# A last fix-up loop in a two-layer graph kernel: its carry moved into one extra tile, weighting and run sums moved, a ring of ten output buffers

## The reference

```python
def _L1_gnn_ref(X, w1, w2, b, edge_weight, edge_src, edge_dst):
    X0 = jnp.einsum('ab,bc->ac', X, w1)
    X1 = jnp.einsum('ab,bc->ac', X, w2)
    msgs = X1[edge_src] * edge_weight[:, None]
    agg = jax.ops.segment_sum(msgs, edge_dst, num_segments=X.shape[0])
    return jax.nn.relu(X0 + agg + b)
...
x = _layernorm(x + _L1_gnn_ref(x, ..., edge_weight, src, dst), axis=-1)
```

## Time and profile before

| | us |
|---|---|
| median of 3 runs | 1562.85 (1562.12 to 1571.67) |
| span of the profiled execution | 1705.3 |
| VectorE busy in it | 1346.5 |
| TensorE busy | 1245.0 |
| ScalarE busy | 1225.0 |
| GpSimd busy | 1042.2 |

### The profile page before, as it was taken

The page is one execution under the profiler, slowest core; times in us unless marked ns, Lnnn a source line. Parts: engine busy times, 40 slices in busy tenths (PEclk is TensorE's granted clock), DMA queues, the critical chain, the costliest instruction groups (busy, mean ns, idle before and its releaser), DMA issues.

```text
span 1705.3 us, 34722 instructions
## 1 busy us (share of the span) xinstructions
PE 1245.0 (73%) x9184; PEld 1095.8 (64%) x9184; DVE 1346.5 (79%) x5156; ACT 1225.0 (72%) x4231; POOL 1042.2 (61%) x1182
## 2 busy tenths in 40 slices
PE   1888888888888882288877876788888876665661
PEld 1877777777777772177766766666666675554551
DVE  2777898889999998888877876799999984654653
ACT  0899999999999995077787876899999962222221
POOL 2666666555566660055555656888888846666665
PEclk9999999999999996599999997999999997787876
DMA  6899999999999996734444445899999942222221
GB/s 189 269 306 302 305 305 304 303 302 301 305 301 305 308 300 233 240 117 152 154 144 140 156 141 168 270 289 292 293 289 294 292 143 77 79 82 74 86 77 38
DMA packets 210148, 372.00 MB, mean 218 GB/s; under 512 B 36740, under 2 KB 67821, under 8 KB 208935
## 3 DMA queue, kind: packets, MB, share of 16 engines
q1 hardware_dynamic: 120822, 200.48, 37.2%
q10 hardware_dynamic: 57771, 108.12, 17.3%
q0 software_dynamic: 31360, 61.17, 13.2%
HBM read 231.39 MB, written 161.37 MB: 230 GB/s over the span
## 4 chain that ended last, share of the span: by engine, by line
ACT 36%; DVE 29%; issue 11%; another core or an unknown queue 9%; PE 9%; DMA 1%; POOL 1%; SPq 1%; DVEq 1%; ACTq 0%; POOLq 0%
ACT hout L728 10%; ACT scan_buf L728 10%; DVE stats L992 7%; DVE hpre L1238 6%; ACT big L756 4%; ACT em L688 3%; DVE big L1228 3%; DVE hpre L1314 2%; ACT lv L769 2%; PE pd L596 2%; DVE hout L1002 2%; DVE scan_buf L1002 2%; PE pd L597 2%; PE pk L619 2%
## 5 line engine op out<-in xcount | busy, mean ns | idle before, releaser
L992 DVE BATCH_NORM_STATS2 stats<-hpre 128x6 f32<-128x256 f32 x882 | 334.8, 421 | 1.8
L466 POOL DMA_INDIRECT ring_a<-in_x,gidx x196 | 185.6, 947 | 207.4 <-PE pt L556 146.7
L728 ACT ACTIVATE scan_buf<-hpre,nb,rs 128x128 f32<-128x128 f32 x686 | 292.1, 480 | 2.8 <-DVE scan_buf L1002 1.3
L728 ACT ACTIVATE hout<-hpre,nb,rs 128x128 f32<-128x128 f32 x686 | 292.2, 480 | 2.5 <-issue 1.2
L1098 DVE SCALAR_TENSOR_TENSOR hpre<-pd,beta,xg 128x128 f32<-128x128 f32 x784 | 221.3, 345 | 29.0 <-DVE beta L1091 1.0
L565 PE MATMUL pd<-w_sx,scan_buf 128*128 128x129 f32 x1568 | 229.7, 276 | 0.0
L469 POOL DMA_INDIRECT ring_b<-in_x,gidx x196 | 185.0, 944 | 60.0 <-issue 60.0
L619 PEld LDWEIGHTS pk<-w_sb,scan_buf 128*128 128x128 f32 x1568 | 211.5, 196 | 7.4
L499 POOL DMA_INDIRECT big<-h_tab,gidx x196 | 193.4, 987 | 35.0 <-POOL big L505 29.5
L619 PE MATMUL pk<-w_sb,scan_buf 128*128 128x128 f32 x1568 | 209.9, 278 | 0.0
L565 PEld LDWEIGHTS pd<-w_sx,scan_buf 128*128 128x128 f32 x1568 | 207.0, 192 | 2.7
(11 more groups left out here) (208 smaller groups left out, 3692.4 us busy)
## 6 DMA issues: line engine op xcount, KB each, us to landing
xg<-in_x SPq DMA_DIRECT2D x196, 256.0 KB
scan_buf<-in_xT SPq DMA_DIRECT2D x196, 256.0 KB
val<-h_tab SPq DMA_DIRECT2D x139, 256.0 KB
h_tab<-hout ACTq DMA_DIRECT2D x98, 256.0 KB
h_tab<-scan_buf ACTq DMA_DIRECT2D x98, 256.0 KB
out_z<-hout ACTq DMA_DIRECT2D x98, 256.0 KB
out_z<-scan_buf ACTq DMA_DIRECT2D x98, 256.0 KB
h_two<-h_tab SPq DMA_DIRECT2D x57, 256.0 KB, 9.1
```

The source lines that it names most:

```text
L466: gp.indirect_dma_start(out=ring_a[:, u, :], out_offset=None, in_=x[:, :], in_offset=bass.IndirectOffsetOnAxis(ap=gidx[:, k, 0:1], axis=0))\
L728: ins = act.activation(hout[ju][:, i * D:(i + 1) * D], hpre[:, ju, i * D:(i + 1) * D], ACT.Identity, bias=nb_of(ju, i), scale=rs_of(ju, i))
L992: ins = dve.bn_stats(stats[:, ju, i, :, :].rearrange("p j s -> p (j s)"), two)
```

## The change

- The carry leaves stage C's loop. The tiles' rows of an inherited run are no longer scattered: `sidx` is raised by 2N where `psame` is 1, so that the bounds check drops them. One **extra tile** at the end computes those rows, at most one for each partition: it gathers the run's last sum from a new DRAM table `agg_scr`, and the h row, adds the scanned carry as a further product into the same PSUM group, and does relu, norm and one scatter.
- `agg_scr` is filled by 49 stores of a quad's sums, on the SP queue, behind the loads of `xg`.
- The weighting goes from GpSimd to ScalarE (`weigh_rows`). The first eight tiles are weighted and summed in the last groups of D2, and the others in stage C's loop, two quads ahead (`KQ = 2`).
- VectorE's order in pass k is now: relu of quad k, run sums of quad k+2, statistics of quad k, normalise quad k-1.
- The normalised quads go round a ring of `UZ = 10` buffers in `val`.
- Semaphores are merged, and small tiles share memory, to make room.

```
-            for k in range(T + GL):
-                if k < T:
-                    if k >= UG:
-                        gp.wait_ge(S["agg_b2"], k - UG + 1)
-                    gp.indirect_dma_start(out=agg[:, k, :], ...)
-                j = k - GL
-                if j >= 0:
-                    gp.wait_ge(hs_in[j % UG], 16 * (j // UG + 1))
-                    gp.tensor_tensor(agg[:, j, :], agg[:, j, :], ew_t[:, j:j + 1].to_broadcast([P, D]),
-                                     ALU.mult).then_inc(S["agg_b2"], 1)
+            for k in range(T):
+                if k >= UG:
+                    gp.wait_ge(hs_in[k % UG], 16 * (k // UG))
+                gp.indirect_dma_start(out=agg[:, k, :], ...).then_inc(hs_in[k % UG], 16)
...
+            for q in range(T4 - 4):
+                scatter_quad(q)
+            gp.wait_ge(S["agg_st"], 16 * T4)
+            gp.indirect_dma_start(out=agg_x, out_offset=None, in_=agg_scr[:, :], ...).then_inc(S["x_in"], 16)
+            gp.indirect_dma_start(out=h_x, out_offset=None, in_=h_tab[:, :], ...).then_inc(S["x_in"], 16)
+            for q in range(T4 - 4, T4):
+                scatter_quad(q)
+            gp.wait_ge(S["sc"], 10)
+            gp.indirect_dma_start(out=out[:, :], ..., in_=z_x, ...).then_inc(S["x_sc"], 16)
...
+            def weigh_rows(t):
+                act.wait_ge(hs_in[t % UG], 16 * (t // UG + 1))
+                act.activation(agg[:, t, :], agg[:, t, :], ACT.Copy, scale=ew_t[:, t:t + 1]).then_inc(S["agg_b2"], 1)
...
+            for k in range(T4 + 1):
+                if k < T4:
+                    if 2 <= k:
+                        c_evict(k)
+                    for t in range(NJ * (k + KQ), min(NJ * (k + KQ + 1), T)):
+                        weigh_rows(t)
+                if k > 0:
+                    inv_std(act, ...)
...
             for k in range(T4 + 1):
-                g = k - 1
                 if k < T4:
...
-                    for i in range(NJ):
-                        t = NJ * k + i
-                        ins = dve.scalar_tensor_tensor(out=hpre[:, ku, i * D:(i + 1) * D], in0=carg, ...)
-                    ins.then_inc(S["cy_c"], 1)
...
+                    dve.scalar_tensor_tensor(out=hpre[:, ku, :], in0=pk[:, k % 2, :], scalar=0.0, in1=xg[:, ku, :],
+                                             op0=ALU.max, op1=ALU.add).then_inc(S["u_c"], 1)
+                    for t in range(NJ * (k + KQ), min(NJ * (k + KQ + 1), T)):
+                        run_sum(t)
                     dve.wait_ge(S["u_c"], k + 1)
                     pair_stats(ku, NJ // 2).then_inc(S["bn_c"], 1)
+                if k > 0:
+                    g = k - 1
+                    dve.wait_ge(S["rs_c"], g + 1)
+                    if g >= UZ:
+                        dve.wait_ge(z_sc[g % UZ], NJ * 16 * (g // UZ))
+                    normalise(lambda i: z_rows(g)[:, i * D:(i + 1) * D], ...).then_inc(S["z_c"], 1)
```

More of the change, by code:

```diff
@@ L27 @@
 NP = 1
+PADDED, FILLS, FILL_E, DROPS, R_O, DSTEPS, ROWS = range(1, 8)
 QSCALE = 1.0 / C ** 0.5
@@ L232, in gnn_kernel @@
         cumT = hpre[:, 1, 0:P + 1]
+        run_a = own[:, 0:D]
+        run_b = own[:, D:2 * D]
+        run_keepT = own[:, 2 * D:3 * D]
+        run_cumT = own[:, 3 * D:4 * D + 1]
+        h_x, agg_x, hT_x, aggT_x = (ring_a[:, i, :] for i in range(4))
+        u_x, z_x = ring_b[:, 0, :], ring_b[:, 1, :]
+        ind = far[:, :]
+        row0 = sb("row0", [P, 1], I32)
+        q_row = q_sb[:, :, :].rearrange("p a n -> p (a n)")
+        at_x = q_row[:, 0:4]
+        rows_x = q_row[:, 8:10].bitcast(I32)
+        stats_x = q_row[:, 16:22].rearrange("p (j s) -> p j s", j=2)
+        lv_x = q_row[:, 24:25]
+        rs_x = q_row[:, 32:33]
         carm = sb("carm", [P, 2 * H])
         fade = sb("fade", [P, 2 * H])
[L235 removed]
+        carn = prod[:, :, :].rearrange("p a n -> p (a n)")[:, 0:DM + H]
         S = {n: sem(n) for n in (
[L239 to L240 removed]
+            "w_in", "pad_in", "ea_cp", "ea_cp2", "z_cp", "edge_in", "setup", "ident", "wprod", "wcopy",
+            "rows_in", "issued", "drop_in", "checked", "ordered",
             "g_all", "g_iota", "g_rank", "ranked", "g_one", "g_ea", "g_out", "g_back", "g_turn",
@@ L281, in gnn_kernel, with z_rows @@
         hv_in = [sem(f"hv_in{i}") for i in range(UV)]
+        z_sc = [sem(f"z_sc{i}") for i in range(UZ)]
+        def z_rows(q):
+            i = UV + q % UZ
+            return val_row[:, i * GN:(i + 1) * GN]
         def h_rows(g):
@@ L507, in _, with scatter_quad @@
+            gp.wait_ge(S["skip_c"], 1)
             for q in range(U):
                 gp.wait_ge(ring["z_st"][q], last)
[L510 to L517, removed]
+            def scatter_quad(q):
+                gp.wait_ge(S["z_c"], q + 1)
+                for i in range(NJ):
+                    k = NJ * q + i
+                    gp.indirect_dma_start(out=out[:, :],
+                                          out_offset=bass.IndirectOffsetOnAxis(ap=sidx[:, k:k + 1], axis=0),
+                                          in_=z_rows(q)[:, i * D:(i + 1) * D], in_offset=None, bounds_check=top_row,
+                                          oob_is_err=False).then_inc(z_sc[q % UZ], 16)
@@ L1294, in _ @@
                     d2_stats(g - 1)
[L1295 to L1301, removed]
+                t = g - (G - NJ * KQ)
+                if 0 <= t:
+                    for i in range(t, NJ * KQ if g == G + 2 else t + 1):
+                        if i < NJ * KQ:
+                            run_sum(i)
```

200 lines of the change are left out of this document (119 added, 81 removed).

## The result

| | before | after |
|---|---|---|
| median of the runs, us | 1562.48 (1561.49 to 1571.67) | 1601.7 (1595.36 to 1609.46) |
| ratio | | 1.023 (1.0181 to 1.0278) |

The change costs 39 us by the medians; the ratio, 1.023, makes it 2.3%, and its interval begins at 1.8%. The forecast of 1564 us was wrong. The outcome lies at the range's upper end of 1600: 1.7 us past it by the median, and 1.2 us inside it if the ratio is applied to the 1562.85 us that the forecast started from. What happened is the rival named *the circle decides*, at 25 in 100.

A forecast was written before the change was run, and what follows sets the result against it. The prediction took GpSimd's scatter issue to bound stage C before and after, with ScalarE left as D2's bound. Terms -5 + 0 + 2 + 3.9 = +1 us on 1562.85 gave 1564 us, range 1535 to 1600 us.

The forecast's parts named there:

- the circle decides: Rival, stage C: lower clock lengthens the loop of waits; 1672 us, or 1585 at one quad in five; 25 in 100 with stutters.
- the weight given to the clock: Stage C: at full clock the loop of waits hides, barely; 2 us added for jitter, ends 0 and +15.
- The circle's own length: Stage C's loop: relu, four sums, four transposes, nine matmuls, two hand-overs; 5.05 us against GpSimd's 5.22 a quad.
- its price at the lower level: Stage C's loop of waits at 1.2 GHz: 7.4 us a quad, +108 us if all quads are at it.
- VectorE no longer runs ahead: Stage C: VectorE gets no lead, so the ten buffers never fill; 2 us for jitter between two equal rates.
- Accident of the profile: Stage C: the first profile's 142.5 us excess likely includes most of C's 50 us, so GpSimd already bounds C in runs.
- D2: Stage D2 and its tail: run sums leave VectorE, ScalarE remains the bound; -5 us, ends 0 and -15.
- Weighting, stores, VectorE's load: Stage C's loop: ScalarE 3.3 us a quad, VectorE +7 us over the stage, stores of 12.8 MB; all hidden.
- the lock: Rival, stage C: VectorE's sums block GpSimd's scatters; 6.7 us a quad, 74 us longer, 1638 us; 3 in 100.
- Ring of ten: Stage C's output buffers: four already hold GpSimd supplied, so ten have nothing to give.
- Extra tile: End of C: two gathers and one scatter more on GpSimd, 3.9 us; its chain lies under the last quad's scatters.
- the start of C: Before C's first scatter: added passes of sums against the carry's saved chain; 0, ends -3 and +5.

The follow-up runs named there:

- e1: The kernel before, unchanged, profiled once more; it took 1559.89 us, with a span of 1558.3 us.
- e3: The changed kernel with twelve unused matmuls put ahead of TensorE's wait for the sums in stage C; 1560.4 us, ratio 0.9963.
- e2: The changed kernel with KQ = 3 instead of 2: weighting, sums and transposes one quad further ahead; 1554.97 us, ratio 0.9937.
- e8: The changed kernel with KQ = 3 and, in D2 from group 49, one of ScalarE's three normalised pieces moved to VectorE; 1544.87 us, ratio 0.9859.
- e7: The changed kernel (KQ = 2) with four output buffers instead of ten (UZ = 4); 1602.48 us, ratio 1.025.
- e4: The changed kernel with weighting back on GpSimd and run sums back on VectorE in D2, as before; 1558.48 us, ratio 0.9957.
- e6: The changed kernel with KQ = 3 and four output buffers instead of ten (UZ = 4); 1558.29 us, ratio 0.9965.

## Why the prediction was wrong, step by step

**The step that failed** is the weight given to the clock: "at full clock it hides, barely", and "two idle us at a time is little beside the 5 to 10 us before which C's clock fell". The circle's own length was right (5.05 us predicted, 5.07 measured), and so was its price at the lower level in kind (7.4 predicted for a quad wholly at it, 6.66 measured: the four transposes and the first steps mostly still ran at the upper one). What was wrong is how often it applies: the range's end took in a quarter of the quads, and it was two thirds. That the time still came out near 1600 is luck: a share far too small was set against a price of 2.2 us a quad, where 1.5 was measured (6.66 against 5.14). I had read in the earlier trace rows that C's clock was at 0.76, and took this for a result of the first profile's long stutters. e1 shows 0.85 without any, where TensorE's idle times (waits for `xg`, 42 times) are 1.3 us on the mean and 2.7 at most. With 2 us of idle in each quad the clock fell again and again (after); with 0.66 us it held 1.00 (e3). But the same 1.97 us stand before quads at either level in after, so these rows do not tell when it falls. The Trainium skill (TensorE: Matmul & The Clock Gate, "A second HAM failure mode: psum-queue depth-cycling") tells of a kernel whose clock swings between its levels because TensorE idles shortly and often between groups of matmuls; the trace of after agrees: 0.82 on the mean, with an idle time of 1.6 to 2 us between one quad's matmuls and the next.

The second half of the same step: I compared mean rates, 5.05 against 5.22, and called the difference hidden. Two rates that close are hidden only while neither changes. In before, with three or four quads of lead, slow quads of TensorE cost nothing (e1 at 0.85). The prediction noted that "VectorE no longer runs ahead" and priced that at 2 us. It was the price of the change. A clock of 0.76 on the mean is the lower level for 48% of the time (some of it at the end, where TensorE had no work: until 1680 us the mean was 0.79). Had I let that row stand and taken it as a share of the quads, the rival's own prices would have given 0.48 x 49 x 2.2 = 52 us, 1616: nearer than 1564, and on the right side.

**The terms that held.**

- *Accident of the profile.* The argument from 142.5 us was right: GpSimd bounded C, and its floor of 256 us is the 255.6 of e1.
- *D2.* ScalarE issues six instructions a group. 260 us hold 738 of them in e1, and 758 in e2, where D2 is as in after: 2.11 and 2.06 us a group, 147 x 0.05 = 7 us. The -5 was right, and so was the reading that ScalarE stays the bound; VectorE was at 82% (214 of 260 us) where some 75% were expected. The limit that I drew at 303 GB/s was none (314 in e8).
- *Weighting, stores, VectorE's load.* Hidden, as said. Scatters took 989 ns with the sums beside them: the lock is not worth 1.5 us a quad (the last section has what there is of it). The row that the prediction held against it was no like case, though: those gathers write their tile into SBUF, and the scatters read theirs from it.
- *Ring of ten.* Nothing, as said (e7).
- *Extra tile.* Its three issues lie where they were expected, 3 x 1.29 us, and its chain lies under the last quad's scatters. But the program's end came sooner by about as much. The last GpSimd issue of e1 begins at 1549.51 and the span ends 8.8 us later; in after:

```profile
1601.75 0.98 POOL L543 DMA_INDIRECT out_z<-val,sidx  x1 [0.31 <-issue]
1603.03 0.98 POOL L560 DMA_INDIRECT out_z<-ring_b,q_sb  x1 [0.30 <-issue]
```

Here it ends 1607.9 - 1603.03 = 4.9 us later. This, with the scatters that are no longer stretched (below), accounts for e4's 8 us: its scatters and the two gathers take 252.9 us in all, against 255.6 in e1. What shortens the end wasn't found. e6 and e7, with a ring of four, have 9.0 and 9.1 us again (e6: 1557.5 - 1548.47), and the kernels with a ring of ten 4.8 to 4.9, so it goes with the ring and not with the tile.

**A smaller term that did not hold** is the start of C, taken at 0 with ends -3 and +5. From D2's last store to the first scatter e1 has 5.9 us (1288.0 to 1293.9), after 12.0 (1291.1 to 1303.1) and e7 12.2: +6 us. In after ScalarE does eight weightings there (from 1291.51 us, 2.45 us) before VectorE has its sums; how the rest is made up wasn't taken apart.

**The sum after the fact**, after's profile against e1's: -8 for D2 (first to last store: 573.7 against 581.8 us), +6 for the start of C, +43 for the scatters' stretch (298.6 - 255.6, in which the extra tile's two gathers stand), -3 for the end: +38 us. The medians differ by 39. The two profiled spans differ by 49.6; the other 11 us lie before D2's first store (717.4 against 706.2 us), where the change does next to nothing and e7, the same but for the ring, has 706.0. Single executions of one kernel differ by 10 us and more.

## What to carry to other kernels

Before a piece of work is moved from a stage into a loop, draw the loop's circle of waits, and ask of every engine in it whether its speed is constant; a circle within a few per cent of the bound is the bound as soon as one engine in it slows down. TensorE, which idled once a quad here, was slower than its full-clock rows say, so price its part at the granted clock that the stage already shows, and read that clock over a window in which it has work. The remedy was distance, not buffers: one iteration more of lead on the input side (`KQ = 3`) gave back 47 us, six buffers more on the output side nothing that could be measured. And when a profiled execution is 9% longer than the runs, profile it again before reading its waits.

## What the runs showed of the hardware

- **The clock falls with short idle times.** 1.97 us of idle in a quad of 5.07 us, again and again: 0.82 on the mean. With 0.66 us of idle: 0.97, and 1.00 until TensorE's loop ended. Twelve matmuls a quad whose results nobody uses made the kernel 41 us faster.
- **The port lock is there, but short.** In e1, 41 scatters begin while VectorE does the relu-and-add (one of them 0.01 us before it), 512 columns with both inputs in SBUF (L1329). VectorE's and GpSimd's timelines of e1, three such places:

```profile
1296.44 0.68 DVE L1329 SCALAR_TENSOR_TENSOR hpre<-hpre,xg 128x512 f32<-128x512 f32 x1
1296.55 1.42 POOL L514 DMA_INDIRECT out_z<-hout,sidx  x1 [0.30 <-issue]
...
1318.46 1.54 POOL L514 DMA_INDIRECT out_z<-hout,sidx  x1 [0.30 <-issue]
...
1318.47 0.68 DVE L1329 SCALAR_TENSOR_TENSOR hpre<-hpre,xg 128x512 f32<-128x512 f32 x1
...
1475.10 0.68 DVE L1329 SCALAR_TENSOR_TENSOR hpre<-hpre,xg 128x512 f32<-128x512 f32 x1
...
1475.57 1.06 POOL L514 DMA_INDIRECT out_z<-scan_buf,sidx  x1 [0.31 <-issue]
```

All three scatters end 0.85 us after the VectorE instruction does (1297.12 and 1297.97; 1319.15 and 1320.00; 1475.78 and 1476.63), and VectorE keeps its 0.68 us. So the end of the scatter waits for the end of that instruction; eight scatters lose 0.35 to 0.57 us, 33 lose up to 0.1 us. In two more places both begin within 0.01 us (1407.56 and 1459.73): there the scatter keeps its 0.97 to 0.98 us, and VectorE takes 0.74 and 0.72. All of e1's scatters together are 6 to 7 us longer than 196 x 0.97. A run sum (both inputs in SBUF as well) lasts 0.35 us; the longest scatter of after took 1.10 us, 0.13 more than 0.97, and all of them together are 3 us longer. The relu of after reads PSUM. The Trainium skill (SBUF — State Buffer, "Who interferes with whom") holds that such a VectorE instruction and a GpSimd operation that reads SBUF shut each other out; e1's rows agree: up to 0.57 us where the scatter was the one that lost, and no more than 0.06 us in the two places where VectorE was. The prediction's price of the rival, the full length of every sum (74 us), was too high: what a scatter loses is less than the rest of the instruction that still runs.
